# Layer 3 of a recommendation tower in four column tiles of TensorE

## The reference

```python
e = jnp.stack([tbl_0[ids[:, 0]], ..., tbl_26[ids[:, 26]]], axis=1)      # 2048 x 27 x 128
interactions = jnp.einsum('bnd,bmd->bnm', inputs, inputs)
i, j = jnp.triu_indices(n, k=1)
z = interactions[:, i, j]                                             # 2048 x 351
h = jnp.concatenate([z, dense_ctx], axis=1)                           # 2048 x 367
h = jnp.maximum(h @ W_top1 + b_top1, 0.0)                             # 512
h = jnp.maximum(h @ W_top2 + b_top2, 0.0)                             # 256
y = h @ W_top3                                                        # 1
```

## Time and profile before

| | us |
|---|---|
| median of 3 runs | 648.5 |
| lowest and highest run | 647.86, 649.17 |
| the profiled execution, whole | 653.6 |
| its span, first to last instruction | 651.4 |
| TensorE's matmuls busy | 385.6 (59% of the span) |
| GpSimd busy | 262.9 (40%) |
| VectorE busy | 190.0 (29%) |
| ScalarE busy | 152.7 (23%) |
| layer 3 (L407), 32 records | 8.5 |
| ScalarE's copies of y (L523), 8 | 5.0 |

### The profile page before, as it was taken

The page is one execution under the profiler, slowest core; times in us unless marked ns, Lnnn a source line. Parts: engine busy times, 40 slices in busy tenths (PEclk is TensorE's granted clock), DMA queues, the critical chain, the costliest instruction groups (busy, mean ns, idle before and its releaser), DMA issues.

```text
span 651.4 us, 8953 instructions
## 1 busy us (share of the span) xinstructions
PE 385.6 (59%) x3952; PEld 340.8 (52%) x3952; DVE 190.0 (29%) x93; ACT 152.7 (23%) x259; POOL 262.9 (40%) x279
## 2 busy tenths in 40 slices
PE   0657204985089821996139951598407973099917
PEld 0546104973079610995029930497306962089815
DVE  1779000850008400272004710075000940027000
ACT  1145001241031400332013320224103241032512
POOL 6773772057600774017730277105770067500000
PEclk9978655996579875899559995699757997589968
DMA  5895220371205621244212731038210682111020
GB/s 129 218 223 136 72 52 21 86 98 52 53 13 96 88 53 39 46 81 82 53 29 55 85 81 52 18 84 98 53 53 6 98 94 53 40 34 37 2 70 0
DMA packets 49375, 44.56 MB, mean 68 GB/s; under 512 B 30304, under 2 KB 43464, under 8 KB 49322
## 3 DMA queue, kind: packets, MB, share of 16 engines
q1 hardware_dynamic: 40634, 26.16, 24.1%
q0 software_dynamic: 8704, 17.84, 10.3%
HBM read 38.00 MB, written 5.98 MB: 68 GB/s over the span
## 4 chain that ended last, share of the span: by engine, by line
PE 55%; issue 36%; DMA 4%; ACT 2%; DVE 2%; SPq 0%; another core or an unknown queue 0%; DVEq 0%
PE gram_ps L369 15%; PE emb_ps L340 11%; PE emb_ps L342 10%; PE mlp_ps L388 7%; PE mlp_ps L398 5%; PE emb_ps L352 5%; DMA gram<-tbl_rows 4%; PE mlp_ps L407 1%; DVE onehot L442 1%; DVE table_lo L457 1%; ACT emb L487 1%; ACT table_hi L469 0%; ACT z L531 0%; ACT h L507 0%
## 5 line engine op out<-in xcount | busy, mean ns | idle before, releaser
L317 POOL DMA_INDIRECT rows<-tbl_rows,idx x272 | 262.1, 964 | 301.4 <-PE emb_ps L352 219.6
L442 DVE TENSOR_TENSOR onehot<-ids_b,row_id 125x2048 fp32r<-125x2048 int32 x80 | 177.9, 2283 | 386.7 <-PE emb_ps L342 360.7
L369 PE MATMUL gram_ps<-emb 128*54 128x54 f32 x2048 | 96.7, 241 | 196.9 <-issue 196.9
L369 PEld LDWEIGHTS gram_ps<-emb 128*54 128x54 f32 x2048 | 82.5, 157 | 214.6 <-issue 214.2
L340 PE MATMUL emb_ps<-onehot,table_hi 125*128 125x256 f32 x640 | 161.9, 293 | 33.9 <-DVE onehot L442 22.7
L342 PE MATMUL emb_ps<-onehot,table_lo 125*128 125x256 f32 x640 | 158.8, 288 | 0.0
L340 PEld LDWEIGHTS emb_ps<-onehot,table_hi 125*128 125x128 f32 x640 | 126.1, 197 | 37.8 <-issue 36.1
L342 PEld LDWEIGHTS emb_ps<-onehot,table_lo 125*128 125x128 f32 x640 | 126.2, 197 | 0.0
L478 ACT COPY emb<-emb_ps 128x512 f32<-128x512 f32 x40 | 32.4, 809 | 119.4 <-PE emb_ps L342 119.4
L487 ACT COPY emb<-emb_ps 128x512 f32<-128x512 f32 (+1 forms) x80 | 44.1, 632 | 68.1 <-remote 51.6
L388 PE MATMUL mlp_ps<-z,w_sb 126*128 126x256 f32 (+1 forms) x192 | 45.9, 398 | 13.2 <-issue 13.2
(11 more groups left out here) (15 smaller groups left out, 20.2 us busy)
## 6 DMA issues: line engine op xcount, KB each, us to landing
ids_b<-ids_onehot SPq DMA_DIRECT2D x16, 640.0 KB
products<-gram SPq DMA_DIRECT2D x32, 182.2 KB
rows<-tbl_rows,idx POOLq DMA_INDIRECT x272
gram<-tbl_rows SPq DMA_DIRECT2D x8, 480.0 KB
z<-products SPq DMA_DIRECT2D x16, 126.0 KB
h<-tbl_rows SPq DMA_DIRECT2D x2, 480.0 KB
w_sb<-w SPq DMA_DIRECT2D x1, 768.0 KB
z<-products SPq DMA_DIRECT2D x8, 96.0 KB
```

The costliest lines, as they stand in the source:

```text
L317: pool.indirect_dma_start(out=rows[:, t, f, :], out_offset=None, in_=gathered_tables[f], in_offset=bass.IndirectOffsetOnAxis(ap=idx[:, p, ...
L369: last = nc.tensor.matmul(ps[half * HALF_ROWS:half * HALF_ROWS + GRAM_COLS, b * GRAM_COLS:(b + 1) * GRAM_COLS], samples, samples, start=Tr ...
L442: nc.vector.tensor_tensor(onehot[0:ROWS, seq % ONEHOT_RING, :, :], ids_b[0:ROWS, k, :].unsqueeze(1).broadcast_to([ROWS, ROWS_PER, PAIR]), ...
```

## The change

Each of layer 3's two matmuls of 256 columns becomes four of 64 columns, one for each quarter q of `h2`'s columns, with the output in partition 32q of the bank, which makes each one a 32-column tile of TensorE of its own. The matmul before was already in such a tile, at partition 0. The loop goes over the halves outside and over the quarters inside. No instruction changes its place among the others on any engine: where TensorE had two of these matmuls in a row it now has eight.

ScalarE now copies partitions 0 to 96 (`Y_ROWS` is 97) with 64 elements each, in their order; of these rows, 0, 32, 64 and 96 hold results and the others are never read. SyncE stores the four rows; the order of the samples is now made by this DMA, whose destination steps by four floats: 4 x 64 single floats.

```diff
+Y_ROWS = P - P // QUARTERS + 1
...
-        y = sb("y", [1, 2, PAIR])
+        y = sb("y", [Y_ROWS, 2, RUN])
...
-                sp.dma_start(out[p * PAIR:(p + 1) * PAIR, :].rearrange("n o -> o n"), y[:, p % 2, :]
+                sp.dma_start(out[p * PAIR:(p + 1) * PAIR, :].rearrange("(g q) o -> q (g o)", q=QUARTERS),
+                             y[0:Y_ROWS:P // QUARTERS, p % 2, :], allow_slow_non_contiguous=True
                              ).then_inc(y_stored[p % 2], 16)
...
                 for k in range(M2):
-                    last = nc.tensor.matmul(ps[0:1, 0:PAIR], w3_sb[:, k:k + 1], h2[:, k, :],
-                                            start=k == 0, stop=k == M2 - 1)
+                    for q in range(QUARTERS):
+                        row = q * P // QUARTERS
+                        last = nc.tensor.matmul(ps[row:row + 1, 0:RUN], w3_sb[:, k:k + 1],
+                                                h2[:, k, q * RUN:(q + 1) * RUN], start=k == 0, stop=k == M2 - 1)
                 last.then_inc(mlp_full, 1)
...
-                nc.scalar.copy(y[:, p % 2, :].rearrange("o (g q) -> o q g", q=QUARTERS),
-                               mlp_ps[chunk % 2][0:1, 0:PAIR].rearrange("o (q g) -> o q g", q=QUARTERS)
-                               ).then_inc(mlp_taken, 1)
+
+                nc.scalar.copy(y[:, p % 2, :], mlp_ps[chunk % 2][0:Y_ROWS, 0:RUN]).then_inc(mlp_taken, 1)
```

## The result

| | us | ratio to before, 95% interval |
|---|---|---|
| kernel before, median of 6 runs beside it | 648.35 | |
| changed kernel, median of 6 runs | 654.76 | 1.0098 (1.0085 to 1.0111) |
| changed kernel, the profiled execution; its span | 654.69; 652.5 | |

The forecast was 646.3 us, with a range from 644.2 to 649.2. The kernel became 1% slower.

The account below looks back on a forecast made before the run. Gathers, a lag, then TensorE alone with layer 3 were taken to bound each pair's loop. Terms: -2.6 us inside, -0.36 tail layer 3, -0.2 copy, +1.0 store, -2.2 from 648.5: 646.3 us, range 644.2 to 649.2.

Parts of the forecast that it names:

- The loop: A pair's turn: gathers 42.1 us, lag 5.8, some 29 of TensorE alone including layer 3; each turn about 0.37 us shorter.
- Layer 3's saving: On TensorE, layer 3 from 0.95 to 0.58 us: 0.37 for each of seven pairs, 2.6 in all, and 0.36 in the tail.
- The factor of 1.75: Overlap of the Gram block's two column tiles, 46 over 26 ns, applied to layer 3's records: 54 to 31 ns each.
- Rival 1: Four tiles abreast on TensorE: layer 3 costs 0.31 us, sum -4.3, 644.2 us; chance 0.10.
- The copy of y: ScalarE's copy takes about 0.41 us for 0.60 to 0.63; off the path seven times, saves 0.2 us in the tail.
- The store in the tail: Last store of y, 256 pieces of 4 bytes on four engines: 0.8 us plus 0.2 for issue, +1.0; bounds 0.3 and 5.0.
- The upper bound of 5.0: Largest cost in us allowed for the tail's store of y, with all pieces on one engine.
- rival 4: Dear store: over 3.2 us more in the tail cancels the gain; 650.3 us with all pieces on one engine; chance 0.08.
- The stores inside the loop: Stores of y before the last pair's: no cost, covered by 3.0 us of SyncE's waiting before the products' store.

Follow-up runs that it names:

- e5: Changed kernel with y's four rows stored as they are and other forms of layer 3 in some pairs; 647.09 us beside 651.82 for the kernel before.
- e6: Changed kernel with y's four rows stored as they are, plus nine test stores of varied patterns behind its end; 256 pieces 64 bytes apart landed in 1.8 us.
- e4_samples_in_order: Changed kernel with ids laid out so each quarter holds 64 consecutive samples and y is stored in rows; first run 409.86 us beside 412.80, ratio 0.994.
- f4_after: The changed kernel, unchanged, on a chip where the kernel before takes 414.15 us; 438.96 us, ratio 1.055.

## Why the prediction was wrong, point by point

- **The loop** was read rightly: gathers, then a lag, then TensorE, with layer 3 on the path. A turn became 0.46 us shorter, forecast were 0.37, and layer 3 itself 0.68 shorter on average in these turns; so about a third of its gain is missing from the loop, and no run shows where it went. This holds for the 650 chips only; on the 413 chips gathers set the pace, and the kernels without pieces are 0.6 to 4.5 us faster in all than the kernel before.
- **Layer 3's saving** was put too low: it took 0.33 us, forecast were 0.58. The factor of 1.75 behind the 0.58 was my estimate from the Gram block's two tiles (46 ns over 26), and no run shows it for four: e5 and the result have 0.33 us with four tiles, e5 0.53 with two and 0.98 with one. The Gram pace fits two tiles abreast as well, and I preferred the reading that let me reuse the factor. Rival 1 (0.31) was the truth, and had a chance of 0.10.
- **The copy of y**: 0.21 us for 0.41, in the right direction.
- **The store in the tail is the step that failed.** I put it at +1.0 us, as 64 pieces for each of four engines at 12 ns. The pieces took 7.1 ns each. But the landing, which I let grow with the packets alone (1.6 us for 0.8) without a row for a small write, is 7.5: +6.7, and +7.0 with the issue. This one term turns the forecast's gain of 2.2 us into a loss. The upper bound of 5.0 was worked out from the wrong quantity, an engine's time, and wasn't a bound. This is rival 4, with another mechanism than the one that I gave it, and a chance of 0.08 was far too low for a resource of which no row existed. What takes the time behind the last packet, no run shows. The size of a piece alone isn't it: pieces 64 bytes apart are as small, and 256 of them land in 1.8 us (e6).
- **The stores inside the loop** were costed at nothing, with the 3 us of SyncE's waiting as their cover. For pairs 0 to 5 that holds on the 650 chips to within about 0.2 us a store. For pair 6 the cover was gone: the last products' store is on the path and came 4 us behind the pieces, +2.0 us. I had counted layer 3 of pair 6 as exposed and not the store that belongs to it.

The sum with measured terms, for the profiles of a 650 chip, is the +4.1 us above. Shown is that the small pieces cause the loss, by their density and through the landing and the last products; why a dense store lands so late, and the 2 us between this sum and the medians, stay open.

`e4_samples_in_order` is the version to keep of those tried: four tiles, no small pieces, in four groups of runs 0.994, 0.9935, 0.996 and 0.988 of the time before, all on 413 chips. On a 650 chip it wasn't run; e5 and e6, with rows and the output's order not restored, were 4 to 7 us faster than before there, in one execution each.

## What to carry to other kernels

A store that scatters single floats is not priced by its packets: look at how long the wait for it is, and at every transfer that follows while it lands (7 to 8 us here). If an order has to be restored, restore it where it is free (here in the layout of the ids), or keep to one or two small pieces in 64 bytes of DRAM, which landed in 1.8 us here. Where the trace has no row for an operation, the upper bound of its cost isn't the nearest row's price times a count.

## What the runs showed that I had not expected

- 256 writes of 4 bytes, 16 of them in each 64 bytes of DRAM, are sent in under 0.5 us and land 7.5 us later; while they do, a packet of the gathers' queue takes 0.64 us of an engine in place of 0.14.
- 32-column tiles of TensorE run abreast in float32 with one column of weights each: 16 records of 64 columns in 0.33 us with four tiles and in 0.98 with one, and 8 records of 128 columns in 0.53 with two.
- The same kernel takes 413 us on two chips and 650 where the result was measured and in one group more. Most of the difference is Gram block 0, which runs in 3.5 us beside gathers on the ones (156.34 to 159.77 in f4_after) and creeps for some 35 us on the other (145.60 to 180.45 in the result's profile).
